# Two half-zero shifts of the first and of the last patch row share one operand

## The chip, the cores and the metric

The kernel runs on one core of a Trainium2 chip. The metric is the device time of one execution in microseconds. The engines are named as in the profile: PE (matrix products), PEld (its weight loads), DVE, ACT, POOL and SP; SP and ACT issue the DMAs.

## What is computed

The reference is a small vision tower. The first stage makes 5 images of 2 channels from each of 64 images of 104 x 104: the image itself and four copies shifted by 4 pixels in both directions and filled with zeros. They are normalised together, multiplied by gamma, moved by beta, and cut into 13 x 13 patches of 8 x 8, each patch giving 128 numbers. A class token is put in front, and two stages follow, of which the attention is a running state over the tokens.

```python
lu, ru, ld, rd = _shifts(x)
concat = jnp.concatenate((x, lu, ru, ld, rd), axis=1)
...
normed = (concat - mean) * jax.lax.rsqrt(var + EPS)
normed = normed * gamma[None] + beta[None]
y = jax.lax.conv_general_dilated(normed, W, window_strides=(PATCH, PATCH), padding='VALID', ...)
...
def step(S, qkv):
    qt, kt, vt = qkv
    S = S + LR * jnp.einsum('bd,be->de', vt, kt)
    out = jnp.einsum('de,be->bd', S, qt)
```

The two upward shifts have zeros in their last 4 pixel rows and the two downward shifts in their first 4. So in the first patch row (tokens 0 to 12) the upper half of a patch is zero in shifts 3 and 4, and in the last patch row (tokens 156 to 168) the lower half is zero in shifts 1 and 2. The last stage of the reference adds one-hot numbers beyond the 128 columns of the tower; here what is left of it is a layer norm that is added.

## The kernel before

**Tiles.** A token is one patch position for all 64 images, so 64 columns. Two tokens are a tile (85 tiles), four tiles a group (22 groups of 8 tokens, the last with one token). The 128 partitions hold the 128 pixels of a patch (2 channels, 64 pixels), in four blocks by quarter of the patch. Thus a half-zero patch is zero in 64 of the 128 partitions.

**Patch stage.** `rows` holds one row of windows in a slot (13 patches of the image itself and 14 shifted by half a patch, of which shifts 1 to 4 take 13 each, from this row or from the one above). `scale_shift` (L378) multiplies one row of one shift by its gammas into `scaled`, a ring of two rows: row 0 on DVE (L1006), all others on POOL (L1097). `conv` (L457) multiplies a piece of up to four tokens of one shift with the weights of that shift, into one of two PSUM banks; five shifts add up, and for groups from 5 on a product with `terms` (L469) adds beta and the image's mean. PE tells by `conv_step` that a shift of a group is done; ACT then copies the bank into `g_t` (`group_out`, L641), and POOL may overwrite the row.

**Head.** SP issues all first loads in one order (L407 to L421): gammas, row 0, the shifted windows above it (`first_offsets`), weights, the small matrices, row 1, beta, the images for the statistics with row 2 among them, and row 3 after DVE's scales of row 0. PE does groups 0 to 3 and part of 4, and the tables (L604) from which `terms` is made. ACT writes the tables to DRAM (`parked`, L767), SP waits for that (L423) and reads them back as `terms` (L427, L428). PE's `early` (L488) needs them; DVE adds its result to `g_t` (`whole`, L782), and ACT's `high` (L651) and POOL's `low` (L1099) split the sum in two parts.

**Steps.** From step -8 to step 71 every engine runs a list of work by step, four steps to a group, written out when the program is built. On PE a step holds the first half of its conv pieces, the three products `vr` (L499) of the tile four ahead, and the second half of the pieces. Every fourth step also has `turn` of the group two ahead (L490), and ends with `products` (L508) and `reads` (L524). On ACT it holds `high`, `values_out` (L665), `rows_out`, `finish`, and last `group_out` of the groups whose last piece lies in the step. `vr` of a tile writes the one bank `vr_ps` and so waits for ACT's `values_out` of the tile before it. On POOL a step holds `low` (first of four), `power` (last of four, L1104), and then the scales; `power(g)` computes 1/sqrt of the variances that DVE gives (L823, L865), and `values_out` of group g waits for it.

**The plan.** `late_item_step` (L86) spreads the 181 late conv pieces from step -8 on; from the 17th on a piece's step goes by the tokens ahead of it, up to step 71. `scale_step` (L134) puts a scale one step behind the last piece that read its place in the ring:

```python
    return int(sum(LATE_COST[sum(FIRST):i]) / sum(LATE_COST[sum(FIRST):]) * CONV_END)
...
    g = last_group_of_row(r - 2)
    steps = [st for (gi, si, _, _), st in zip(LATE_ITEMS, ITEM_STEPS) if gi == g and si == s]
    return 1 + max(steps)
```

After step 71 comes a tail written out by hand (L559). Its first `vr` and `turn` follow the last conv pieces directly.

Of the kernel before, what the change touches and what calls it, by code (L numbers as in the profile page):

```python
# [11 lines left out]
P = 128  # L12
B = 64
E = 128
S = 104
# [42 lines left out]
def tokens_of(g):  # L58
    return range(TOKENS * g, min(TOKENS * g + TOKENS, PATCHES))
# [5 lines left out]

def pieces(g):

    cuts, out = [tokens_of(g)[0], tokens_of(g)[-1] + 1], []
    cuts[1:1] = [t for t in tokens_of(g)[1:] if t % RING == 0]
    for a, z in zip(cuts, cuts[1:]):  # L70
        mid = a + (z - a + 1) // 2 if z - a > 4 else z
        out += [(a, mid - a)] + ([(mid, z - mid)] if mid < z else [])
    return out


def conv_items(g):
    return [(g, s, a, n) for s in range(SHIFTS) for a, n in pieces(g)]

# [63 lines left out]

LATE_SCALES = [(r, s, scale_step(r, s)) for r in range(EARLY_ROWS, N) for s in range(SHIFTS)]


def tower(nc, x_rows, x_windows, first_offsets, gamma, beta, weight, smalls, cls_tok, out, parked):
    with ExitStack() as ctx:
        def sb(name, shape, dtype=F32):
            return ctx.enter_context(nc.sbuf_tensor(name, shape, dtype))
# [4 lines left out]
        def sem(name):  # L154
            return ctx.enter_context(nc.semaphore(name))
# [4 lines left out]
        bet = sb("bet", [P, SHIFTS, PATCHES])  # L160
        wt = sb("wt", [P, SHIFTS, E])
        small = sb("small", [P, 8, E])
# [70 lines left out]
        gamma_in = sem("gamma_in")  # L233
        weight_in = sem("weight_in")
        beta_in = sem("beta_in")
        first_offsets_in = sem("first_offsets_in")
# [141 lines left out]
        def scale_shift(eng, r, s):  # L378
            offsets = (r if s < 3 else r - 1) % ROW_SLOTS
            right = N + (s - 1) % 2  # L380
            window = rows[:, r % ROW_SLOTS, 0:N] if s == 0 else rows[:, offsets, right:right + N]
            gains = gam[:, s, r * N:r * N + N].unsqueeze(2).to_broadcast([P, N, B])
            at = r % 2 * N
            return eng.tensor_tensor(scaled[:, s, at:at + N], window, gains, ALU.mult)  # L384
# [4 lines left out]
        def _(sp):  # L389
# [16 lines left out]

            sp.dma_start(gam[:], gamma).then_inc(gamma_in, 16)  # L407
            load_row(0)
            sp.dma_start(rows[:, ROW_SLOTS - 1, N:2 * N + 1], first_offsets).then_inc(first_offsets_in, 16)
            sp.dma_start(wt[:], weight).then_inc(weight_in, 16)  # L410
            sp.dma_start(small[:], smalls).then_inc(small_in, 16)
# [7 lines left out]

            sp.wait_ge(scaled_first, SHIFTS)  # L420
            load_row(3)  # L421
            sp.wait_ge(terms_zero, 1)
            sp.wait_ge(terms_parked, 32)  # L423
# [32 lines left out]
        def _(pe):  # L456
            def conv(item):  # L457
                g, s, a, n = item
                if s == 0 and a == tokens_of(g)[0] and g >= 2:
                    pe.wait_ge(g_ready, g - 1)  # L460
                wait_scaled(pe, s, a, n)
                at, first = (a - tokens_of(g)[0]) * B, s == 0 and a == tokens_of(g)[0]
                last = pe.matmul(conv_ps[g % 2][:, at:at + n * B], wt[:, s], scaled[:, s, a % RING:a % RING + n],  # L463
                                 start=first, stop=(g < EARLY and s == SHIFTS - 1), skip_group_check=True)
                if a + n == tokens_of(g)[-1] + 1:
                    last.then_inc(conv_step, 1)
                    if s == SHIFTS - 1 and g >= EARLY:
                        cols = len(tokens_of(g)) * B
                        pe.matmul(conv_ps[g % 2][:, 0:cols], terms[:, g], own_scales[:, 0:cols], start=False, stop=True,  # L469
                                  skip_group_check=True).then_inc(group_done, 1)  # L470
# [125 lines left out]
            pe.matmul(first_ps[:, 0:E], wq_c[:], small[:, MEM], start=True, stop=False, skip_group_check=True)  # L596
            pe.wait_ge(gamma_in, 16)
            pe.wait_ge(beta_in, 16)
# [182 lines left out]
        def _(dve):  # L781
# [221 lines left out]

            dve.wait_ge(gamma_in, 16)
            dve.wait_ge(row_in[0], 16)
            for s in range(SHIFTS):  # L1006
                if s == 3:
                    dve.wait_ge(first_offsets_in, 16)
                scale_shift(dve, 0, s).then_inc(scaled_first, 1)
# [81 lines left out]
        def _(pool):  # L1091
            def scale(r, s):
                if s == 0:
                    pool.wait_ge(row_in[r % ROW_SLOTS], 16 * (r // ROW_SLOTS + 1))
                if r >= 2:
                    pool.wait_ge(conv_step, SHIFTS * last_group_of_row(r - 2) + s + 1)
                scale_shift(pool, r, s).then_inc(scaled_rows, 1)  # L1097

# [57 lines left out]
            pool.tensor_tensor(cls_rho[:], cls_var[:], powers[:, 0:1], ALU.pow).then_inc(rho_ready, 1)  # L1156
            pool.wait_ge(gamma_in, 16)
            for r in range(1, EARLY_ROWS):
# [58 lines left out]
```

## Time and profile before

| | |
|---|---|
| median of 3 runs | 227.39 us (227.32 to 227.43) |
| the profiled execution | 227.42 us, of it 225.6 us from the first to the last instruction (span) |
| PE | busy 198.7 us, 88% |
| DVE | busy 152.6 us, 68% |
| ACT | busy 114.0 us, 51% |
| POOL | busy 160.1 us, 71% |
| conv products (L463) | 460 records, two for a piece, 116.0 us |
| scales on POOL (L384) | 60, 93.8 us, 1587 ns each |

The profile comes from one execution. A busy time is that of an engine's own instructions; waiting isn't counted. Products on PE overlap in their records, so what one costs is read from the chain of work, where the pieces follow one another without overlap. An idle time is written in brackets behind an instruction with what ended it. Of a chain, each piece is followed back from the last instruction to what released it.

### The profile page before, as it was taken

Reading aid. Unit: us, or ns where it says so; the run is one execution under the profiler, and the core shown is the slowest. Engines: PE = TensorE matmul, PEld = TensorE weight load, DVE = VectorE, ACT = ScalarE, POOL = GpSimd, SP = SyncE. Lnnn points to the kernel's source line nnn. Section 1 sums busy time; section 2 is a strip of 40 time slices with the busy share of each in tenths; the row PEclk is TensorE's granted clock in tenths of the full one; section 3 lists DMA queues with packets and bytes.
Section 4 is the critical chain, followed back from the end, with each engine's and each line's share of the span. In section 5 each row is a group of like instructions: output and inputs, shape, how many; then the busy total and the mean of one; then the engine's idle time right before and its main releaser. Section 6 shows DMA issues by size and latency. Waiting matters only on the chain.

```text
span 225.6 us, 4908 instructions
## 1 busy us (share of the span) xinstructions
PE 198.7 (88%) x1558; PEld 169.4 (75%) x1558; DVE 152.6 (68%) x752; ACT 114.0 (51%) x252; POOL 160.1 (71%) x126
## 2 busy tenths in 40 slices
PE   0299997899899999999999999999999999998700
PEld 0289896778788899888888888899888888887500
DVE  2558984251666876677695786588667769688771
ACT  6003211245344454656745666574567566467971
POOL 1039969899983799968999759849999353263550
PEclk9999999999999999999999999999999999999955
DMA  6999966922204004243044422022102202202255
GB/s 165 367 437 416 422 256 105 349 113 51 109 0 161 3 0 165 47 148 105 5 120 130 160 49 46 3 48 49 45 2 49 48 3 48 46 4 46 49 116 124
DMA packets 16527, 26.00 MB, mean 115 GB/s; under 512 B 1303, under 2 KB 13261, under 8 KB 16246
## 3 DMA queue, kind: packets, MB, share of 16 engines
q1 hardware_dynamic: 15820, 25.18, 34.9%
q10 hardware_dynamic: 682, 0.51, 0.7%
q8 instruction: 13, 0.21, 0.4%
q14 instruction: 12, 0.10, 0.1%
HBM read 19.77 MB, written 5.92 MB: 114 GB/s over the span
## 4 chain that ended last, share of the span: by engine, by line
PE 65%; DMA 12%; POOL 10%; DVE 6%; issue 2%; ACT 2%; POOLq 1%; SPq 0%; DVEq 0%; ACTq 0%
PE conv L463 29%; DMA rows<-x_windows 12%; PE vr_ps L505 11%; PE outs L532 9%; PE first_ps L515 8%; POOL scaled L384 7%; PE turn L495 4%; DVE scaled L384 2%; PE conv L469 2%; POOL g_low L1101 1%; PE conv L505 1%; ACT values L668 1%; POOL rstd L1111 1%; DVE state L811 1%; DVE state L803 1%
## 5 line engine op out<-in xcount | busy, mean ns | idle before, releaser
L463 PE MATMUL conv<-scaled,wt 128*128 128x256 f32 (+3 forms) x460 | 116.0, 372 | 9.9 <-DMA wt<-weight 9.9
L384 POOL TENSOR_TENSOR scaled<-rows,gam 128x832 f32<-128x832 f32 x60 | 93.8, 1587 | 6.3 <-PE conv L463 4.1
L463 PEld LDWEIGHTS conv<-scaled,wt 128*128 128x128 f32 x460 | 77.2, 193 | 18.0 <-DMA wt<-weight 9.9
L668 ACT ACTIVATE values<-vr_ps,rstd 128x256 f32<-128x256 f32 x78 | 36.9, 474 | 65.1 <-PE vr_ps L505 54.9
L1111 POOL TENSOR_TENSOR rstd<-var,powers 128x8 f32<-128x8 f32 (+2 forms) x20 | 30.4, 1519 | 23.9 <-DVE var L823 23.9
L803 DVE TENSOR_TENSOR state<-first_ps,state 128x128 f32<-128x128 f32 x80 | 23.3, 291 | 30.9 <-PE first_ps L515 26.1
L676 ACT ACTIVATE images<-images,ln_shift,ln_gain 128x128 f32<-128x128 f32 x82 | 38.0, 488 | 1.6 <-DVE ln_shift L874 1.6
L505 PE MATMUL vr_ps<-w_high,g_low 128*128 128x256 f32 x80 | 32.1, 401 | 0.2 <-ACT values L668 0.2
L1101 POOL TENSOR_TENSOR g_low<-g_t,g_high 128x512 fp32r<-128x512 f32 x21 | 26.8, 1275 | 5.1 <-ACT g_high L655 4.3
L792 DVE BATCH_NORM_STATS2 ln_stats<-images 128x6 f32<-128x128 f32 x85 | 23.7, 284 | 6.9 <-ACT images L662 6.7
L811 DVE TENSOR_TENSOR state<-second_ps,state 128x128 f32<-128x128 f32 x80 | 22.6, 282 | 2.1
L515 PEld LDWEIGHTS first_ps<-values 64*128 64x128 f32 x160 | 19.3, 187 | 6.2 <-issue 5.9
L515 PE MATMUL first_ps<-values 64*128 64x128 f32 x160 | 23.1, 284 | 0.2 <-ACT values L668 0.2
L518 PE MATMUL second_ps<-values 64*128 64x128 f32 x160 | 23.1, 285 | 0.0
L505 PE MATMUL vr_ps<-w_low,g_high 128*128 128x256 f32 x80 | 22.5, 281 | 0.0
L505 PE MATMUL vr_ps<-w_high,g_high 128*128 128x256 f32 x80 | 22.4, 280 | 0.0
L649 ACT COPY g_t<-conv 128x512 f32<-128x512 f32 (+1 forms) x22 | 12.3, 560 | 19.2 <-PE conv L463 19.2
L532 PE MATMUL outs<-state,g_t 128*64 128x128 f32 x304 | 20.8, 279 | 0.0
L832 DVE SCALAR_TENSOR_TENSOR images<-outs,rstd,images 128x128 f32<-128x128 f32 x72 | 20.4, 342 | 0.0
L505 PEld LDWEIGHTS vr_ps<-w_high,g_low 128*128 128x128 f32 x80 | 15.1, 189 | 6.1 <-issue 4.6
L518 PEld LDWEIGHTS second_ps<-values 64*128 64x128 f32 x160 | 19.3, 187 | 0.0
L840 DVE BATCH_NORM_STATS2 ln_stats<-images 128x6 f32<-128x128 f32 x85 | 18.9, 278 | 0.2 <-POOL images L1116 0.2
(149 smaller groups left out, 240.3 us busy)
## 6 DMA issues: line engine op xcount, KB each, us to landing
rows<-x_windows SPq DMA_DIRECT2D x13, 864.0 KB, 5.7
out<-images SPq DMA_DIRECT2D x40, 128.0 KB, 2.4
images<-x_rows SPq DMA_DIRECT2D x3, 624.0 KB, 22.0
images<-x_rows SPq DMA_DIRECT2D x1, 1456.0 KB, 13.1
images<-x_rows SPq DMA_DIRECT2D x1, 1248.0 KB, 15.5
images<-x_rows SPq DMA_DIRECT2D x1, 832.0 KB, 19.6
small<-smalls SPq DMA_DIRECT2D x1, 512.0 KB, 8.6
terms<-parked SPq DMA_DIRECT2D x3, 168.0 KB
```

The source lines that it names most:

```text
L384: return eng.tensor_tensor(scaled[:, s, at:at + N], window, gains, ALU.mult)
L463: last = pe.matmul(conv_ps[g % 2][:, at:at + n * B], wt[:, s], scaled[:, s, a % RING:a % RING + n], start=first, stop=(g < EARLY and s == ...
L505: last = pe.matmul(vr_bank(t)[:, 0:2 * E], x[:, at:at + E], w[:], start=(i == 0), stop=(i == 2))
L515: first = pe.matmul(first_bank[:, at:at + E], values[0:B, slot, 0], values[0:B, slot, 1], start=True, stop=True, skip_group_check=True)
L518: second = pe.matmul(second_bank[:, at:at + E], values[B:P, slot, 0], values[B:P, slot, 1], start=True, stop=True, skip_group_check=True)
L532: last = pe.matmul(out_bank(g)[a:a + B, at:at + E], g_t[:, g % G_SLOTS, at + a:at + a + B], state[:, t % STATE_SLOTS, half], start=True, s ...
L668: act.activation(values[:, t % VALUE_SLOTS].rearrange("p a e -> p (a e)"), vr_bank(t)[:, 0:2 * E], ACT.Identity, scale=rho_of(t)).then_inc ...
L676: return act.activation(tile_of(result, OUT_SLOTS, t), tile_of(h2, H2_SLOTS, t), ACT.Identity, scale=gain_of(t), bias=shift_of(t))
L803: dve.tensor_tensor(state[:, t % STATE_SLOTS, 0], banks_of(t)[0][:, at:at + E], state[:, (t - 1) % STATE_SLOTS, 1], ALU.add).then_inc(stat ...
L811: dve.tensor_tensor(state[:, t % STATE_SLOTS, 1], banks_of(t)[1][:, at:at + E], state[:, t % STATE_SLOTS, 0], ALU.add).then_inc(state_read ...
L1101: pool.tensor_tensor(low_of(g), g_t[:, g % G_SLOTS, 0:len(tiles_of(g)) * E], high_of(g), ALU.subtract).then_inc(low_ready, 1)
L1111: pool.tensor_tensor(rstd[:, g, 0:cols], var[:, g, 0:cols], powers[:, 0:cols], ALU.pow).then_inc(rho_ready, 1)
```

## The change

For tokens 0 to 12 shifts 3 and 4 are put together: their nonzero halves (64 partitions each) make one operand of 128 partitions, prepared on the host in `first_offsets`; a gamma row and a sixth set of weights are put together to match. For tokens 156 to 168 the same is done with shifts 1 and 2 (in the last row of `x_windows`, with a seventh set of weights). So these 26 tokens take four products instead of five. The pieces of shift 4 for the first row and of shift 2 for the last are gone, with one scale on DVE and one on POOL; some pieces are cut at token 13. The plan of pieces and scales is computed anew from the shorter list. SP issues two more DMAs: the put-together gammas (128 x 26 numbers) as the second of all, and the seventh set of weights (64 KB) behind row 3; the first load of weights has six sets instead of five. The waits on `gamma_in` count two loads, and PE waits on `bottom_in` before products with the seventh set. `conv_step` and `scaled_rows` count by two where one shift is gone.

```diff
@@ -63,10 +63,25 @@
-def pieces(g):
-
-    cuts, out = [tokens_of(g)[0], tokens_of(g)[-1] + 1], []
-    cuts[1:1] = [t for t in tokens_of(g)[1:] if t % RING == 0]
+TOP, BOTTOM = 3, 1
+LAST_ROW = N * (N - 1)
+
+
+def pieces(g, s):
+
+
+    a, z = tokens_of(g)[0], tokens_of(g)[-1] + 1
+    if s == TOP + 1:
+        a = max(a, N)
+    if s == BOTTOM + 1:
+        z = min(z, LAST_ROW)
+    if a >= z:
+        return []
+    cuts, out = [a, z], []
+    cuts[1:1] = [t for t in range(a + 1, z) if t % RING == 0 or (s == TOP and t == N)]
     for a, z in zip(cuts, cuts[1:]):
         mid = a + (z - a + 1) // 2 if z - a > 4 else z
         out += [(a, mid - a)] + ([(mid, z - mid)] if mid < z else [])
@@ -74,7 +89,7 @@
 def conv_items(g):
-    return [(g, s, a, n) for s in range(SHIFTS) for a, n in pieces(g)]
+    return [(g, s, a, n) for s in range(SHIFTS) for a, n in pieces(g, s)]
@@ -140,10 +155,11 @@
-LATE_SCALES = [(r, s, scale_step(r, s)) for r in range(EARLY_ROWS, N) for s in range(SHIFTS)]
+LATE_SCALES = [(r, s, scale_step(r, s)) for r in range(EARLY_ROWS, N) for s in range(SHIFTS)
+               if (r, s) != (N - 1, BOTTOM + 1)]
@@ -158,7 +174,8 @@
-        wt = sb("wt", [P, SHIFTS, E])
+        wt = sb("wt", [P, SHIFTS + 2, E])
+        gam_edges = sb("gam_edges", [P, 2, N])
@@ -379,7 +397,10 @@
-            gains = gam[:, s, r * N:r * N + N].unsqueeze(2).to_broadcast([P, N, B])
+            gains = gam[:, s, r * N:r * N + N]
+            if (r, s) in ((0, TOP), (N - 1, BOTTOM)):
+                gains = gam_edges[:, 1 if r else 0]
+            gains = gains.unsqueeze(2).to_broadcast([P, N, B])
@@ -405,9 +426,10 @@
             sp.dma_start(gam[:], gamma).then_inc(gamma_in, 16)
+            sp.dma_start(gam_edges[:], gamma_edges).then_inc(gamma_in, 16)
             load_row(0)
-            sp.dma_start(rows[:, ROW_SLOTS - 1, N:2 * N + 1], first_offsets).then_inc(first_offsets_in, 16)
-            sp.dma_start(wt[:], weight).then_inc(weight_in, 16)
+            sp.dma_start(rows[:, ROW_SLOTS - 1, N:2 * N], first_offsets).then_inc(first_offsets_in, 16)
+            sp.dma_start(wt[:, 0:SHIFTS + 1], weight[:, 0:SHIFTS + 1]).then_inc(weight_in, 16)
@@ -417,8 +439,9 @@
-            sp.wait_ge(scaled_first, SHIFTS)
+            sp.wait_ge(scaled_first, SHIFTS - 1)
             load_row(3)
+            sp.dma_start(wt[:, SHIFTS + 1], weight[:, SHIFTS + 1]).then_inc(bottom_in, 16)
@@ -460,10 +483,14 @@
-                last = pe.matmul(conv_ps[g % 2][:, at:at + n * B], wt[:, s], scaled[:, s, a % RING:a % RING + n],
-                                 start=first, stop=(g < EARLY and s == SHIFTS - 1), skip_group_check=True)
+                held = SHIFTS if s == TOP and a < N else SHIFTS + 1 if s == BOTTOM and a >= LAST_ROW else s
+                if held == SHIFTS + 1:
+                    pe.wait_ge(bottom_in, 16)
+                last = pe.matmul(conv_ps[g % 2][:, at:at + n * B], wt[:, held], scaled[:, s, a % RING:a % RING + n],
+                                 start=first, stop=(g < EARLY and (s == SHIFTS - 1 or held == SHIFTS)), skip_group_check=True)
                 if a + n == tokens_of(g)[-1] + 1:
-                    last.then_inc(conv_step, 1)
+
+                    last.then_inc(conv_step, 2 if (g, s) == (0, TOP) else 1)
@@ -1001,10 +1028,10 @@
-            dve.wait_ge(gamma_in, 16)
+            dve.wait_ge(gamma_in, 32)
             dve.wait_ge(row_in[0], 16)
-            for s in range(SHIFTS):
-                if s == 3:
+            for s in range(TOP + 1):
+                if s == TOP:
                     dve.wait_ge(first_offsets_in, 16)
                 scale_shift(dve, 0, s).then_inc(scaled_first, 1)
@@ -1094,7 +1121,7 @@
-                scale_shift(pool, r, s).then_inc(scaled_rows, 1)
+                scale_shift(pool, r, s).then_inc(scaled_rows, 2 if (r, s) == (N - 1, BOTTOM) else 1)
@@ -1187,6 +1214,17 @@
+    x_windows = np.concatenate([patches, offsets[:, 1:]], axis=2)
+    half = P // 2
+    x_windows[half:P, N - 1, N:2 * N] = offsets[0:half, N, 1:N + 1]
+    first_offsets = offsets[:, 0, 0:N].copy()
+    first_offsets[0:half] = offsets[half:P, 0, 1:N + 1]
```

## Rows read from the trace of the kernel before

**Rows 1.** Busy by stretch: PE, PEld, DVE, ACT, POOL; then PE clock, DMA share, GB/s.
```profile
66.00:196.00 130.00, 130.00 (x1079) 111.33 (x1077) 95.33 (x514) 75.15 (x167) 100.12 (x68) 1.00 0.23 64
...
27.00:42.00 15.00, 12.76 (x71) 11.16 (x70) 8.66 (x27) 2.05 (x5) 12.82 (x9) 1.00 0.73 214
```

**Rows 2.** Chain of work that ended last, the head: start us, us, what.
```profile
8.04 4.78 DVE scaled L384 x5
...
12.83 20.82 DMA rows<-x_windows
...
42.13 0.97 issue
```

**Rows 3.** PE's timeline and SP's wait before the first steps.
```profile
41.18 0.50 PE L488 MATMUL turn<-own_scales,terms 128*128 128x512 f32 x1 [0.92 <-DMA terms<-parked]
...
SPq L423 <- DMA parked<-term_parts: 22.0, 1, 22.0
```

**Rows 4.** The chain at the end of the loop, steps 69 to 72.
```profile
194.33 1.06 PE conv L463 x4
...
195.74 0.43 PE conv L463 x2
196.18 0.23 PE conv L469
196.41 0.61 PE conv L463 x6
197.02 0.41 PE vr_ps L505 x3
...
197.91 0.49 PE turn L495 x4
...
198.80 0.48 ACT values L668
...
199.41 0.34 PE first_ps L515
```

**Rows 5.** PE's timeline in the head: first product, and the wait for sums.
```profile
9.95 0.79 PE L463 MATMUL conv<-scaled,wt 128*128 128x256 f32 x1 [9.95 <-DMA wt<-weight]
...
34.67 0.38 PE L621 MATMUL outs<-sums,small 128*128 128x2 f32 x2 [0.40 <-DVE sums L1060]
```

**Rows 6.** Stretches in the head, columns as in rows 1; ACT queue's packets, MB, share.
```profile
9.00:14.00 5.00, 4.05 (x10) 3.25 (x11) 4.96 (x13) 0.00 (x0) 0.00 (x0) 1.00 1.05 434
...
31.60:33.70 2.10, 2.10 (x17) 2.10 (x16) 2.07 (x7) 0.59 (x1) 0.00 (x0) 1.00 0.12 49
...
q10 hardware_dynamic: 224, 0.03, 1.9%
```

**Rows 7.** POOL's timeline in the first burst of scales; DVE's variance before it.
```profile
74.89 1.58 POOL L384 TENSOR_TENSOR scaled<-rows,gam 128x832 f32<-128x832 f32 x1 [3.63 <-PE conv L463]
76.43 1.79 POOL L1111 TENSOR_TENSOR rstd<-var,powers 128x9 f32<-128x9 f32 x1
...
94.58 1.63 POOL L1111 TENSOR_TENSOR rstd<-var,powers 128x8 f32<-128x8 f32 x1
...
75.98 0.28 DVE L823 TENSOR_SCALAR var<-dve,powers,moments 128x4 f32<-128x4 f32 x1
```

**Rows 8.** ACT's wait for power; vr(25) in the chain; two starts after a wait.
```profile
96.31 0.47 ACT L668 ACTIVATE values<-vr_ps,rstd 128x256 f32<-128x256 f32 x1 [1.84 <-POOL rstd L1111]
...
97.90 0.35 PE vr_ps L505 x3
...
206.09 0.59 PE conv L505 x3
...
60.58 0.65 PE L495 MATMUL turn<-small,g_t 128*128 128x128 f32 x4 [0.64 <-DVE g_t L786]
```

**Rows 9.** ACT's timeline in step 69.
```profile
196.15 0.48 ACT L676 ACTIVATE images<-images,ln_shift,ln_gain 128x128 f32<-128x128 f32 x1
196.54 0.57 ACT L649 COPY g_t<-conv 128x512 f32<-128x512 f32 x1
```

More of the change, by code:

```diff
@@ L140, in scale_step, with tower @@
     return 1 + max(steps)
-LATE_SCALES = [(r, s, scale_step(r, s)) for r in range(EARLY_ROWS, N) for s in range(SHIFTS)]
-def tower(nc, x_rows, x_windows, first_offsets, gamma, beta, weight, smalls, cls_tok, out, parked):
+LATE_SCALES = [(r, s, scale_step(r, s)) for r in range(EARLY_ROWS, N) for s in range(SHIFTS)
+               if (r, s) != (N - 1, BOTTOM + 1)]
+def tower(nc, x_rows, x_windows, first_offsets, gamma, gamma_edges, beta, weight, smalls, cls_tok, out, parked):
     with ExitStack() as ctx:
@@ L234, in tower @@
         weight_in = sem("weight_in")
+        bottom_in = sem("bottom_in")
         beta_in = sem("beta_in")
@@ L596, in _ @@
             pe.matmul(first_ps[:, 0:E], wq_c[:], small[:, MEM], start=True, stop=False, skip_group_check=True)
-            pe.wait_ge(gamma_in, 16)
+            pe.wait_ge(gamma_in, 32)
             pe.wait_ge(beta_in, 16)
@@ L1156, in _ @@
             pool.tensor_tensor(cls_rho[:], cls_var[:], powers[:, 0:1], ALU.pow).then_inc(rho_ready, 1)
-            pool.wait_ge(gamma_in, 16)
+            pool.wait_ge(gamma_in, 32)
             for r in range(1, EARLY_ROWS):
@@ L1189 @@
             offsets[q:q + 32, 1 - a:1 - a + N, 1 - b:1 - b + N] = patches[src:src + 32]
+    x_windows = np.concatenate([patches, offsets[:, 1:]], axis=2)
[3 more added lines that the diff above has]
+    first_offsets[0:half] = offsets[half:P, 0, 1:N + 1]
+    gains = windows(gamma.reshape(SHIFTS, 2, S, S)).reshape(P, SHIFTS, PATCHES)
+    weight = w.reshape(E, SHIFTS, 2, 2, HALF, 2, HALF).transpose(3, 5, 2, 4, 6, 1, 0).reshape(P, SHIFTS, E)
+    gain_edges = [np.concatenate([gains[half:P, TOP + 1, 0:N], gains[half:P, TOP, 0:N]]),
+                  np.concatenate([gains[0:half, BOTTOM, LAST_ROW:], gains[0:half, BOTTOM + 1, LAST_ROW:]])]
+    weight_edges = [np.concatenate([weight[half:P, TOP + 1], weight[half:P, TOP]]),
+                    np.concatenate([weight[0:half, BOTTOM], weight[0:half, BOTTOM + 1]])]
     smalls = np.zeros((P, 8, E), np.float32)
@@ L1198 @@
         "x_rows": x.reshape(P, S, S),
-        "x_windows": np.concatenate([patches, offsets[:, 1:]], axis=2),
-        "first_offsets": offsets[:, 0],
-        "gamma": windows(gamma.reshape(SHIFTS, 2, S, S)).reshape(P, SHIFTS, PATCHES),
+        "x_windows": x_windows,
+        "first_offsets": first_offsets,
+        "gamma": gains,
+        "gamma_edges": np.stack(gain_edges, axis=1),
         "beta": windows(beta.reshape(SHIFTS, 2, S, S)).reshape(P, SHIFTS, PATCHES),
-        "weight": w.reshape(E, SHIFTS, 2, 2, HALF, 2, HALF).transpose(3, 5, 2, 4, 6, 1, 0).reshape(P, SHIFTS, E),
+        "weight": np.concatenate([weight, np.stack(weight_edges, axis=1)], axis=1),
         "smalls": smalls,
```

## Prediction, made before the changed kernel was run

> **What bounds the kernel now.** I read the page's busy shares first, then busy time by stretch, then the chain of work that ended last, then the timelines of single engines where the change touches them. The picture has three parts. From 66 to 196 us PE is busy in 130.00 of 130.00 us [rows 1]: what is taken off PE there comes off the time, as long as nobody makes PE wait. Before that PE has gaps (12.76 of 15.00 us from 27 to 42) [rows 1], and the chain starts from DMA: row 3 of the windows lands at 12.83 + 20.82 = 33.65 us, and POOL scales it [rows 2]. The piece to look at is the 0.97 us from 42.13: POOL has finished its scales and stands for the first `g_high`. That comes from PE's first `early` product at 41.18 us, which waited 0.92 us for the DMA of `terms`, and SP could issue that DMA only after 22.0 us of waiting for the `parked` writes [rows 3]. So the landing of `parked` and `terms` sets the start of the steps, and row 3 has some 1.0 us to spare behind it. The third part, after 196 us, starts from PE's last turns and `vr` products and follows them one to one.
>
> **Head, PE and DVE.** Group 0 loses its two products of shift 4; group 1 loses one and gets smaller ones. A piece of 4 tokens costs 0.43 us [rows 4], 0.107 a token, so 13 tokens are 1.4 us of PE. DVE loses one scale (five took 4.78) [rows 2], and as `cls_var` comes behind them, POOL starts row 1 some 0.95 us earlier. None of it reaches the start: PE then waits longer for `sums` at 34.67 us [rows 5], which hangs on the last image chunk, and POOL waits longer for row 3. I count zero. The cover is the DMA stream; without it this would be worth up to 1.4 us.
>
> **Head, DMA.** SP's queue gets a load of 13 KB in 104-byte pieces ahead of row 0, 64 KB more weights ahead of `small`, and 32 KB less of `first_offsets`: 45 KB more ahead of the images and row 3, at 434 GB/s [rows 6] 0.1 us. The nearest row for small packets are the 224 packets of the ACT queue: 1.9% of 16 engines over 10 us, 13.6 ns each [rows 6]; 8 per engine are 0.1 us. The Trainium skill (DMA: Bandwidth & Descriptors, Specifications) wants at least 512 B for line rate and calls anything less a read-modify-write; it gives no price for one, and the row above says that these are cheap. Row 0 is issued one slot later, but the gamma load ahead of it is still in flight then. The other 64 KB (the weights for row 12) are queued behind row 3 and meet the `parked` writes. From 31.6 to 33.7 us only 49 GB/s flow, at a DMA share of 0.12: about two of the 16 engines still work off a backlog [rows 6]. If the load spreads over 16, a late engine gets 4 KB more, 0.16 us at 49/2 GB/s. If all 64 KB had to pass at 49 GB/s, it would be 1.3 us. I take 0.3 for the whole, bounds 0.1 and 1.5. It stands in front of `terms`, so it is paid in full. Row 3 is issued after four scales instead of five, but it spends 20.8 us in the queue anyway: nothing.
>
> **Loop, PE.** The planner spreads the late pieces evenly by tokens up to step 71: 669 tokens and 181 pieces before, 656 and 177 after; three pieces of four tokens and one of one token vanish. By both plans, worked out from the code, 12 tokens are gone by the start of step 69: 3 x 0.43 = 1.29 us, in a stretch where PE has no gap. This is the gain. The single token goes in step 70.
>
> **Loop, POOL.** The plan also moves POOL's scales, whose step is that of a conv piece plus one. (6,0) goes from step 10 to step 11, where it stands behind `power(4)` in POOL's order. Before, it ran at 74.89 us, in the time before DVE gave the variance of group 4 (75.98 + 0.28), and POOL was then busy without a gap until `power(6)` ended near 96.18 us [rows 7]. Up to that `power` the instructions are the same before and after; only the start differs. PE is 0.43 us ahead by then (step 7 has one piece less), so `power(4)` starts at 75.85 and the pair is done at 79.15 instead of 78.21, and `power(6)` ends 0.94 us later, at 97.12. ACT's `values` of tile 24 waited 1.84 us for it already and began at 96.31 [rows 8]. After: 97.25, done 97.72, seen by PE 0.13 later (ACT's end 199.28 to PE's 199.41 [rows 4]) at 97.85. `vr(25)` ran from 97.90 for 0.35 us [rows 8]; 0.43 earlier it would end at 97.82. Starting at 97.85 after a wait it ends at 98.44 (three took 0.59 so [rows 8]). So PE stands about 0.62 us, with all of step 21 queued behind it, and as PE has no gap later, nothing makes it up. Bounds 0 (POOL gets its variance earlier than I think) and 0.9. The other bursts: (8,0) also goes a step later, but its piece lies in the first half of step 24, and `power(10)` comes 0.4 us later, within the 0.65 us or so that `vr(25)` had beyond the longest wait of before; rows 10 to 12 have fewer scales ahead of their powers than before. Zero for these. (12,2) is gone, 1.54 us of POOL near 165 us, where PE is the bound: nothing.
>
> **End of the loop.** The last piece of group 20 moves from step 69 to step 70. ACT's order in step 70 is `values(74)`, then the copies of groups 20 and 21. PE's is that piece, the bias product, two single tokens, `vr(74)`, two single tokens, then `turn(20)`, which needs the copy of group 20. So the copy comes behind `vr(74)`; before, it ran at 196.54 [rows 9], while `vr(74)` ended at 197.43 [rows 4]. From the start of step 69 to the end of that turn it was 197.91 + 0.49 - 194.33 = 4.07 us [rows 4]. After, by the same rows: 0.63 (half of the two pieces at 194.33, with the start after reads), 0.35 and 0.43 for step 69; 0.43, 0.23, 0.41 (two of three single tokens in 0.61) and 0.41 to the end of `vr(74)`; 0.04 to ACT, 0.39 to the copy (one step on ACT [rows 9]), 0.57 for it, 0.13 to PE, and 0.65 for a turn after a wait [rows 8]. Sum 4.67: 0.60 longer, where 0.21 shorter was to be had. Bounds -0.21 and 0.7. Behind the turn comes `vr(75)`, then `values(75)` at 198.80, for which PE stood before 199.41 [rows 4], so the tail takes it in full.
>
> **The sum.** The profiled execution took 227.42 us, span 225.6 and 1.8 around it; the median of the runs is 227.39, and 0.03 is not worth a correction. 227.42 + 0.3 (DMA) - 1.29 (pieces) + 0.62 (`power(6)`) + 0.60 (step 70) = 227.65.
>
> **The rivals.** A measurement of this kernel can tell about 0.2%, 0.45 us, from no change; "same" is 226.95 to 227.85.
> First, the forecast: the two new waits and the DMA eat the pieces. 227.65. Chance 0.45.
> Second, the gain arrives. Both waits rest on differences of half a microsecond; with neither, 227.42 - 1.49 + 0.1 = 226.0; with the step-70 wait alone and 0.3 of DMA 227.0, and 226.6 with half of it. For it: PE stood nowhere in 130 us though ACT waited up to 1.84 us for `power` [rows 1, 8]. Against it: both waits follow from the order of the instructions. Chance 0.27.
> Third, slower: the 64 KB behind row 3 hold up the `parked` writes. The place is the thin stream after 31.6 us, the price up to 1.3 us instead of 0.16, and it decides from a start that comes 0.5 us later: 227.42 + 1.5 - 1.29 + 0.62 + 0.60 = 228.85, at half the price 228.3. For it: the stream is thin because few engines carry it [rows 6]. Against it: the weights can spread over all 16. Chance 0.22.
> Fourth, PE's rate. The first product after 9.95 us of rest took 0.79 us [rows 5], nearly twice the 0.43 that two of them take later, and the change leaves PE without work for about 1.8 us before `sums` (0.40 before), longer than the 0.92 before `early` [rows 3, 5]. At half rate the six pieces after `sums` (16 tokens) take 3.4 us instead of 1.7 and the four after them as much again; they end near 42.3 us, some 1.1 after the landing of `terms`: 228.75. The Trainium skill (TensorE: Matmul & The Clock Gate, Part 1) says that an idle array falls to half its 2.4 GHz clock and gets it back only after sustained work; the profile's own column grants 1.00 from 9 to 14 us as elsewhere [rows 1, 6], so the trace shows the long product and not its cause. Chance 0.03.
> Fifth, it does less than it says: a piece's price is that of its two weight loads, not of its tokens. Pieces of four at 0.43 against single tokens at 0.20 [rows 4] speak against it; with 4 late pieces less at 0.20 the sum is 228.1. Chance 0.03.
>
> **How the numbers follow.** Slower: 0.22, 0.03 and 0.03, less what of the third lies under 227.85: 0.27. Faster: 0.26 of the second's 0.27. Same: 0.47. The range goes from half of the step-70 wait to half the price of the slower rival, about 1 in 10 outside at either end.
>
> **What would show it.** Right: PE's first gap in the loop is near 97 us, at `vr` and for ACT's `values`, 0.3 to 0.9 us, with ACT waiting about 3.2 us for `rstd` (1.84 + 0.94, and PE 0.43 earlier); `turn(20)` waits for ACT's copy about 0.65 us; `early(0)` starts between 41.3 and 41.8 us; conv pieces take 2.8 us less in all. Wrong: `early(0)` at 42 us or later (third); PE without a gap from 66 us to the last turn (second); conv products near 0.8 us after `sums` (fourth). The forecast as a whole is wrong if the copy of group 20 runs ahead of `vr(74)`, or if `power(4)` finds its variance ready.

## The result and the profile after

The changed kernel takes 229.84 us (median of 22 runs, 228.07 to 232.36) where the kernel before takes 227.30 us beside it (22 runs, 227.19 to 227.91): the ratio is 1.0098, 95% interval 1.0079 to 1.0117. Two of its runs (231.87 and 232.36 us) lie over 1.5% above its fastest, count as slow and are left out of the ratio. It is slower by 1%, outside the predicted range (226.6 to 228.3 us), and its times spread over 4 us where those of before spread over 0.7. The profiled execution took 230.41 us, span 228.6: 2.99 us more than that of before.

The page of the profile after gives, as engine, busy time, share of the span and instructions, and as the granted clock by slices in tenths:

```profile
PE 198.0 (87%) x1546; PEld 168.2 (74%) x1546; DVE 152.2 (67%) x751; ACT 113.8 (50%) x252; POOL 158.6 (69%) x125
PEclk9999999799999999999999999999999999999975
```

PE and POOL have less work than before (198.7 and 160.1 us), so the loss is not work. The eighth slice of the clock, a 7, is the stretch from 40.0 to 45.7 us; it was a 9 before. The chain of work that ended last (start, us, what) shows where it lies:

```profile
5.81 12.81 DMA images<-x_rows
...
18.64 3.42 DVE dve L1066 x8
22.06 1.24 DVE w_low L1069
...
27.25 9.09 DMA parked<-term_parts
...
38.28 4.94 DMA terms<-parked
43.27 0.79 PE turn L515
...
64.04 0.66 PE turn L522 x4
...
101.17 0.57 PE vr_ps L532 x3
...
196.86 0.63 PE conv L489 x2
```

Of before, the same turn starts at 60.58 [rows 8] and the same pieces at 194.33 [rows 4]. So the kernel is 3.46 us late at the turn, has won back 0.93 at the pieces with which step 69 begins (2.53 late), and loses 0.5 in step 70. The whole question is the head. PE's timeline there (start, us, line, operation, partitions and elements; idle before in brackets), and then one line of before:

```profile
35.04 0.38 PE L648 MATMUL outs<-sums,small 128*128 128x2 f32 x2 [1.03 <-DVE sums L1087]
...
43.27 0.79 PE L515 MATMUL turn<-own_scales,terms 128*128 128x512 f32 x1 [3.41 <-DMA terms<-parked]
43.86 2.61 PE L489 MATMUL conv<-scaled,wt 128*128 128x256 f32 x6
```

```profile
41.52 1.46 PE L463 MATMUL conv<-scaled,wt 128*128 128x256 f32 x6
```

`early(0)` starts at 43.27 instead of 41.18, after 3.41 us of waiting for `terms` instead of 0.92 [rows 3]. And the six products behind it take 2.61 us; the same six took 1.46 before. The view by microsecond (length; busy us and instructions of PE, PEld, DVE, ACT and POOL; granted clock, DMA share, GB/s) says why:

```profile
42.00:43.00 1.00, 0.00 (x0) 0.00 (x0) 0.00 (x0) 0.00 (x0) 0.00 (x0) 0.88 0.76 194
43.00:44.00 1.00, 0.73 (x2) 0.64 (x3) 0.00 (x0) 0.00 (x0) 0.00 (x0) 0.50 0.94 387
...
45.00:46.00 1.00, 1.00 (x4) 0.72 (x4) 0.00 (x0) 0.44 (x1) 0.48 (x1) 0.50 0.99 408
46.00:47.00 1.00, 1.00 (x8) 0.89 (x7) 0.00 (x0) 0.06 (x1) 1.00 (x2) 0.91 1.06 436
```

From 43 to 46 us PE is granted 0.50, which is the lower of its two levels (1.2 of 2.4 GHz), after its long rest. The lateness of 3.46 us at the turn is thus 2.09 from the later start of `early(0)` and 1.37 from what follows it. The Trainium skill (TensorE: Matmul & The Clock Gate, Part 1) says that an idle array falls to half its 2.4 GHz clock; the trace agrees, with 0.50 granted after 3.41 us of rest.

The later start has two parts. The first `terms` load is issued 1.23 us later (35.20 and 36.43), behind a `parked` that was issued 1.41 us later (25.47 before, 26.88 after). From there to `early(0)` it takes 6.84 us instead of 5.98, 0.86 more. The second is the surprise: nothing in the change touches that transfer. Of the first, about 1 us is not seen in every execution: e4_warm and e7_plan below have the same head up to that point, and there the load is issued at 35.41 and 35.56. Why it came at 36.43 here (and at 36.29 in e2_late) stays open.

### The profile page after: what moved, and what is told of

Read it like the earlier page. It is cut to its first block, busy times and chain, and to the rows that moved or that the text cites. A ratio compares the mean times of both kernels' runs of the same rounds, so it can differ in the third digit from the quotient of the medians.

```text
span 228.6 us, 4888 instructions
## 1 busy us (share of the span) xinstructions
PE 198.0 (87%) x1546; PEld 168.2 (74%) x1546; DVE 152.2 (67%) x751; ACT 113.8 (50%) x252; POOL 158.6 (69%) x125
## 4 chain that ended last, share of the span: by engine, by line
PE 65%; DMA 12%; DVE 8%; POOL 5%; SPq 3%; ACT 3%; issue 2%; POOLq 1%; DVEq 0%; ACTq 0%
PE conv L489 29%; PE vr_ps L532 11%; PE outs L559 9%; PE first_ps L542 8%; DMA images<-x_rows 6%; DMA parked<-term_parts 4%; PE turn L522 4%; DVE dve L1066 3%; POOL scaled L405 3%; DMA terms<-parked 2%; PE conv L496 2%; PE conv L532 1%; POOL rstd L1138 1%; ACT values L695 1%; DVE state L838 1%
## 5 line engine op out<-in xcount | busy, mean ns | idle before, releaser
L489 PE MATMUL conv<-scaled,wt 128*128 128x256 f32 (+3 forms) x448 | 114.8, 375 | 10.8 <-DMA wt<-weight 10.8
L405 POOL TENSOR_TENSOR scaled<-rows,gam 128x832 f32<-128x832 f32 x58 | 90.5, 1583 | 2.9 <-DMA rows<-x_windows 1.5
L489 PEld LDWEIGHTS conv<-scaled,wt 128*128 128x128 f32 x448 | 75.7, 195 | 18.9 <-DMA wt<-weight 10.8
```

The lines of the kernel that those rows point to most:

```text
L489: last = pe.matmul(conv_ps[g % 2][:, at:at + n * B], wt[:, held], scaled[:, s, a % RING:a % RING + n], start=first, stop=(g < EARLY and (s ...
```

## The experiments

In all tables here "issue" is SP's issue of the first `terms` load, and "early" the start of `early(0)`. Ratios are to the kernel before, run beside each, with the 95% interval; they are not those of the two medians. A time inside a kernel is that of its one profiled execution.

| | median us (range, runs) | ratio | issue to early | PE's rest before it |
|---|---|---|---|---|
| before | 227.30 (227.19–227.91, 22) | | 35.20 → 41.18: 5.98 | 0.92 |
| after | 229.84 (228.07–232.36, 22) | 1.0098 [1.0079, 1.0117] | 36.43 → 43.27: 6.84 | 3.41 |
| e1_fold | 228.81 (227.51–230.71, 12) | 1.0068 [1.0043, 1.0093] | 35.47 → 42.32: 6.85 | 2.13 |
| e2_late | 228.28 (227.76–230.96, 12) | 1.0061 [1.0034, 1.0087] | 36.29 → 43.27: 6.98 | 2.83 |
| e3_fold_late | 229.38 (227.66–230.15, 12) | 1.0077 [1.0055, 1.0100] | 35.32 → 42.37: 7.05 | 2.08 |
| e4_warm | 228.59 (228.44–228.86, 5) | 1.0056 [1.0044, 1.0068] | 35.41 → 42.65: 7.24, not all of it the load | none |
| e5_before_edges | 229.09 (228.04–231.37, 9) | 1.0091 [1.0054, 1.0127] | 35.28 → 42.43: 7.15 | 1.89 |
| e6_before_bottom | 227.38 (226.85–227.58, 11) | 1.0001 [0.9993, 1.0010] | 35.16 → 41.15: 5.99 | 0.87 |
| e7_plan | 228.93 (227.56–230.08, 7) | 1.0068 [1.0040, 1.0096] | 35.56 → 42.56: 7.00 | 2.17 |
| e8_all | 227.88 (227.26–229.34, 12) | 1.0047 [1.0028, 1.0066] | 35.32 → 42.24: 6.92 | 2.00 |
| f1_sbuf | 229.28 (227.99–230.32, 7) | 1.0083 [1.0053, 1.0113] | 35.13 → 42.44: 7.31 | 2.43 |
| f2_dram | 227.31 (227.08–227.59, 11) | 1.0000 [0.9991, 1.0008] | 35.14 → 41.15: 6.01 | 0.93 |
| f3_all_sbuf | 226.75 (226.29–226.83, 7) | 0.9970 [0.9959, 0.9980] | 35.26 → 41.23: 5.97 | 0.87 |
| f4_all_both | 226.18 (226.12–226.80, 5) | 0.9962 [0.9949, 0.9974] | 35.29 → 41.17: 5.88 | 0.99 |
| g1_pad | 227.28 (227.16–227.44, 11) | 1.0003 [0.9994, 1.0011] | 35.72 → 41.53: 5.81 | 1.24 |
| g2_pad_plan | 226.88 (226.72–226.99, 11) | 0.9983 [0.9975, 0.9992] | 35.48 → 41.44: 5.96 | 1.48 |
| g3_shift256 | 227.22 (227.18–227.40, 11) | 1.0001 [0.9992, 1.0009] | 35.13 → 40.96: 5.83 | 0.69 |
| g4_terms_only | 229.74 (227.97–230.56, 6) | 1.0098 [1.0068, 1.0128] | 35.10 → 41.79: 6.69 | 1.70 |

### The two added transfers, taken away one by one

The first suspects were the two new loads. e1_fold puts the 26 gammas behind the others, in one tile and one load; e2_late moves the weights for the last row behind row 4, after all of `terms`; e3_fold_late does both.

```diff
-        gam = sb("gam", [P, SHIFTS, PATCHES])
-        gam_edges = sb("gam_edges", [P, 2, N])
+        gam_all = sb("gam_all", [P, SHIFTS * PATCHES + 2 * N])
...
-            sp.dma_start(gam[:], gamma).then_inc(gamma_in, 16)
-            sp.dma_start(gam_edges[:], gamma_edges).then_inc(gamma_in, 16)
+            sp.dma_start(gam_all[:], gamma).then_inc(gamma_in, 16)
```

> The changed kernel, with the 13 KB of put-together gammas appended to the gamma load, so that no small DMA stands second in SP's queue. Theory A (the small DMA holds back the first loads: row 0 landed 0.8 us later, the first images 0.8 us later, DMA moved 55 GB/s from 4 to 5 us instead of 248; through the tables and the parked writes this delays terms, and PE rests until its clock falls): row 0 lands at 8.0 us again, early(0) starts near 41.5 us, no stretch at half clock, 227.2 to 227.6. Rival B (the 64 KB behind row 3 hold up the parked writes): no change, 229.8. Rival C (the longer wait for terms is chance of the DMA, not tied to an edit): 228 to 232 again.

```diff
             load_row(3)
-            sp.dma_start(wt[:, SHIFTS + 1], weight[:, SHIFTS + 1]).then_inc(bottom_in, 16)
...
             load_row(4)
+            sp.dma_start(wt[:, SHIFTS + 1], weight[:, SHIFTS + 1]).then_inc(bottom_in, 16)
```

> The changed kernel, with the 64 KB of weights for the last row loaded behind row 4, after the terms, instead of behind row 3. Theory A (small DMA ahead of row 0): parked done at 36.4 us as before, early(0) near 43 us, 229.5 or more. Rival B (these 64 KB hold up the parked writes): parked lands 0.5 to 1.2 us earlier, early(0) near 41.8 us, 227.8 to 228.3.

> Both edits of e1_fold and e2_late. Theory A: as e1_fold within 0.3 us, 227.0 to 227.6. Rival B: as e2_late. If both matter, clearly under either: the head is that of the kernel before, and the time is 227.4 - 1.3 + 0.2 (power) + 0.5 (step 70) = 226.8.

All three stay slower than before. e2's median lies where its rival B put it (227.8 to 228.3), but not for B's reason: B wanted `early(0)` near 41.8, and it comes at 43.27. The fold brings row 0 at 8.16 instead of 8.84. `terms` is issued 0.96 us earlier than in after; that this is the fold's doing isn't shown, since e4_warm, without the fold, issues it at 35.41 too. And `early(0)` comes only at 42.32, since the transfer itself takes 6.85 us. With both loads out of the way (e3), issue stands at 35.32, as good as before's 35.20, and `early(0)` is still 1.19 us late.

### The clock

e4_warm gives PE ten products whose result is not used, just ahead of the wait for `terms`; the rest is after.

```diff
+            for _ in range(10):
+                pe.matmul(vr_ps[:, 2 * E:3 * E], wq_c[:], small[:, MEM], start=True, stop=True, skip_group_check=True)
             pe.wait_ge(terms_in, 16 * 2 * PRODUCTS)
```

> The changed kernel, with ten products of 128 columns that nobody reads on PE before its wait for terms, some 2.2 us of work in a rest of 3.4 us. If the fall of the clock after that rest is a part of the loss (0.50 granted from 43 to 46 us, three pieces in 2.6 us instead of 1.5), then no stretch at half clock, and 1.1 to 1.4 us less: 228.4 to 228.7, with less spread. If the clock cost nothing because DVE or POOL was late anyway: 229.8.

PE's timeline of e4_warm:

```profile
40.50 2.40 PE L660 MATMUL vr_ps<-small,wq_c 128*128 128x128 f32 x20
...
42.65 0.48 PE L515 MATMUL turn<-own_scales,terms 128*128 128x512 f32 x1
42.96 1.46 PE L489 MATMUL conv<-scaled,wt 128*128 128x256 f32 x6
```

The products are at the upper level again, 1.46 us for six instead of 2.61, and the spread of the times is gone: 0.4 us over five runs instead of 4. So the halved clock is real, and without it the spread is gone, in these five runs. Yet the kernel is still 0.56% slower than before: the late `terms` is not explained by the clock. e4 also starts `early(0)` 0.62 us sooner than after does, since its `terms` is issued at 35.41. It pays something of its own as well: `early(0)` follows the unused products without idle time, and the last of the six loads lands at 42.16, so about half a microsecond of its 7.24 is those products and not the load, which takes 6.75.

### One part alone, on the kernel before

e5_before_edges gives the kernel before the small gamma tile and its load, which nobody reads (the waits on `gamma_in` count it, as in the changed kernel); e6_before_bottom gives it 64 KB of weights behind row 3.

```diff
+        gam_edges = sb("gam_edges", [P, 2, N])
...
+            sp.dma_start(gam_edges[:], gamma_edges).then_inc(gamma_in, 16)
```

> The kernel before, with one more DMA of 13 KB (104 bytes a partition) second in SP's queue, which nothing uses. Theory A (it holds back the first loads and so terms): row 0 lands 0.8 us later, early(0) 1 to 2 us later, the clock falls in some executions, 228.5 to 231 with a spread of 2 us or more. Rival B (the other load is to blame): 227.4, no spread.

```diff
+        wt_more = sb("wt_more", [P, E])
...
             load_row(3)
+            sp.dma_start(wt_more[:], weight[:, SHIFTS]).then_inc(bottom_in, 16)
```

> The kernel before, with one more DMA of 64 KB behind row 3, which nothing uses. Theory A: 227.3 to 227.6. Rival B (it holds up the parked writes): 0.5 to 1.5 us more, 227.9 to 228.9.

```profile
42.43 0.50 PE L490 MATMUL turn<-own_scales,terms 128*128 128x512 f32 x1 [1.89 <-DMA terms<-parked]
```

```profile
41.15 0.50 PE L491 MATMUL turn<-own_scales,terms 128*128 128x512 f32 x1 [0.87 <-DMA terms<-parked]
```

The first line is of e5, the second of e6. The 64 KB cost nothing: 41.15 against 41.18. The small tile brings nearly the whole loss, 0.91% of 0.98%. But e5 issues `terms` at 35.28, on time; it is again the transfer that takes 7.15 us. A load of 13 KB from the start of the kernel, over 25 us earlier, is hardly in its way. What the tile leaves behind is 104 bytes a partition, 128 as the tiles are laid out, and all tiles behind it move up by them.

### The plan

e7_plan is after with the pace of the late pieces as it was before, so that every scale, and every piece up to group 18, has the step that it had before; e8_all has it along with fold and late load.

```diff
-CONV_END = 71
+CONV_END = 71 * 592 / 605
```

> The changed kernel, with the plan's end scaled down with the tokens (71 x 592 / 605 = 69.5), so that every piece up to group 18 and every scale has the step it had in the kernel before, and group 20 is done in step 68. If the new steps cost 0.2 us at vr(25) and 0.5 at turn(20), as the trace of the changed kernel reads: 0.7 to 0.8 us less than the changed kernel, 229.1, with no wait of PE for ACT's copy and none for power near step 21. If that time comes back elsewhere: 229.8.

> The changed kernel with the gammas in one load, the last weights behind row 4 and the scaled plan. Sum of the parts: 227.4 for the head of before, less 1.3 to 1.5 for the pieces, no new waits: 225.9 to 226.2. If the head stays late from another cause (64 KB more weights ahead of the images): 226.5 to 227.5.

e8_all misses its 225.9 to 226.2 by 1.7 us. Both kernels still have the late `terms`; e8_all, in an execution where the clock didn't fall (2.00 us of rest, 1.00 granted), reached 227.26. What the plan is worth shows only in g2_pad_plan, below.

### Where a tile lies

Worked out from the order of the tiles, `terms` starts 180224 bytes into a partition before, a multiple of 512, and 181376 after, 128 bytes beyond one. A partition's row of one `terms` load is 512 bytes. f1_sbuf is the kernel before with 104 unused bytes, and no load. f2_dram leaves the tiles alone and makes the gammas' array in DRAM as much longer.

```diff
         bet = sb("bet", [P, SHIFTS, PATCHES])
+        unused = sb("unused", [P, 2 * N])
```

> The kernel before, with 104 bytes a partition of SBUF set aside behind beta and used by nothing, so that the tiles behind it (weights, small matrices, scaled, terms and the rest) lie 104 bytes higher, as in the changed kernel. In the seven profiles so far with such a shift, terms came 6.8 to 7.2 us after SP's issue; in the two without, 6.0. Theory D (the place of the tiles in SBUF sets the DMA's pace): terms 6.8 us or more after issue, PE's rest about 1 us longer, 227.8 to 229 with more spread, with no added DMA at all. Rival E (the place of parked in DRAM, or the added DMA): 227.3.

> The kernel before, with the gamma array in DRAM 13 KB longer (104 bytes a partition, not loaded), so that what lies behind it in DRAM is moved as in the changed kernel. Rival E (place in DRAM): terms 6.8 us or more after issue, 227.8 or more. Theory D (place in SBUF): 6.0 us, 227.3.

```profile
35.13 0.33 SPq L428 DMA_DIRECT2D terms<-parked  x1
```

```profile
42.44 0.56 PE L489 MATMUL turn<-own_scales,terms 128*128 128x512 f32 x1 [2.43 <-DMA terms<-parked]
42.80 2.76 PE L464 MATMUL conv<-scaled,wt 128*128 128x256 f32 x6
```

This is f1: a program that does exactly what before does, with 104 bytes between two tiles, loses 0.83%. `terms` is issued at 35.13 and lands 7.31 us later; the six products behind it take 2.76 us. f2 is at 1.0000. DMA share and GB/s by microsecond (after the comma: granted clock, share, GB/s), first of f1, then of before:

```profile
37.00:38.00 1.00, 1.00 1.18 115
38.00:39.00 1.00, 1.00 1.28 104
39.00:40.00 1.00, 1.00 1.28 90
40.00:41.00 1.00, 1.00 1.55 143
```

```profile
37.00:38.00 1.00, 1.00 0.97 170
38.00:39.00 1.00, 1.00 1.28 116
39.00:40.00 1.00, 1.00 1.52 184
40.00:41.00 1.00, 1.00 0.75 207
```

Over the four microseconds the DMA engines are busier in f1 (mean share 1.32 against 1.13) and move less (113 GB/s against 169). The packets themselves say it most plainly. The six loads are 1014 packets of 512 bytes; in the DMA records of f1 one takes 74 ns on average, in those of before 52.

g4_terms_only leaves the tiles ahead of `terms` where they were and puts `terms` 104 bytes further (to 128 beyond a multiple of 512, since this kernel's tiles start at multiples of 32). Its expectation says that every other tile keeps its place against 512; that isn't quite so. The 408 bytes behind `terms` take 416, and `term_parts` and what follows it start 32 bytes beyond such a multiple. g3_shift256 moves it, and all behind, by 256 bytes. g1_pad is after with the small tile made 512 bytes long, of which 104 are used.

```diff
+        unused = sb("unused", [P, 26])
         terms = sb("terms", [P, GROUPS, E], F32R)
+        unused_too = sb("unused_too", [P, E - 26])
```

> The kernel before, with 104 unused bytes ahead of terms and 408 behind it: terms alone starts 128 bytes beyond a multiple of 512, every other tile keeps its place against 512. If terms is the tile that matters: 6.8 us or more from issue to early(0), 228 to 230 as in f1_sbuf. If it is another tile (small, weights, scaled, rows of values): 6.0 us and 227.3.

```diff
         bet = sb("bet", [P, SHIFTS, PATCHES])
+        unused = sb("unused", [P, 64])
```

> The kernel before, with 256 unused bytes a partition behind beta, so that weights, terms and the rest start 256 bytes beyond a multiple of 512. If a row must not straddle a multiple of 512: terms 6.8 us or more after issue and 228 to 230, as in f1_sbuf (128 beyond). If multiples of 256 are enough: 6.0 us and 227.3.

```diff
-        gam_edges = sb("gam_edges", [P, 2, N])
+        gam_edges = sb("gam_edges", [P, E])[:, 0:2 * N].rearrange("p (k t) -> p k t", t=N)
```

> The changed kernel with one edit: the tile of the put-together gammas takes 512 bytes a partition instead of 104, so that terms and all behind it start at a multiple of 512 bytes again (181760 instead of 181376; 181376 is 128 more than such a multiple). Nothing else moves, the small DMA stays. Theory D (512-byte rows that straddle a multiple of 512): terms 6.0 us after SP's issue instead of 6.8. Row 0 and the tables are still late, so early(0) near 42.2 us, 227.6 to 228.2; if the clock still falls in some executions, spread. Rival A (the small DMA makes all of the loss): 229.8.

`early(0)` in g4, g3 and g1, one fence each, and behind g1's the six products:

```profile
41.79 0.50 PE L490 MATMUL turn<-own_scales,terms 128*128 128x512 f32 x1 [1.70 <-DMA terms<-parked]
```

```profile
40.96 0.50 PE L489 MATMUL turn<-own_scales,terms 128*128 128x512 f32 x1 [0.69 <-DMA terms<-parked]
```

```profile
41.53 0.50 PE L515 MATMUL turn<-own_scales,terms 128*128 128x512 f32 x1 [1.24 <-DMA terms<-parked]
41.87 1.46 PE L489 MATMUL conv<-scaled,wt 128*128 128x256 f32 x6
```

Moving `terms` gives the whole loss (1.0098, the ratio of after). The 32 bytes of the tiles behind it don't touch the six loads, which come from DRAM and write `terms`; `parked`, which is written from `term_parts`, goes out at 25.36 and lets `terms` be issued at 35.10, as early as in any kernel here. The profiled execution of g4, at 227.97 us the fastest of its six, kept the clock at 1.00 and so shows the price of the late landing by itself: 0.61 us. The other 1.8 us of its median (229.74) came in executions of which there is no trace; after's trace puts 1.37 us on the clock, and some 0.4 us of g4 stay untraced. A shift of 256 bytes costs nothing (1.0001), and g1 takes the whole loss off the change: 1.0003, better than the 227.6 to 228.2 us expected of it. In the table all runs in which `terms` starts 96 or 128 bytes beyond a multiple of 256 (after, e1 to e5, e7, e8, f1, g4) need 6.69 to 7.31 us from issue to `early(0)`, and all others 5.81 to 6.01. Their 512-byte packets take 62 to 74 ns on average, those of the others 48 to 52. The Trainium skill (DMA: Bandwidth & Descriptors, How a descriptor splits into AXI transactions) says of reads that a transaction must start at a multiple of 256 bytes, and that a transfer which starts between two of them fetches bytes that it doesn't use. Taken over to the writes here, that would make three transactions of a 512-byte row instead of two, an estimate. The runs agree in where the border lies (96 and 128 cost, 256 doesn't); they don't show transactions, nor does the page give a price in time.

### What the change is worth with its tile in place

f3_all_sbuf is e8_all with the gamma tile lengthened to keep `terms` at a multiple of 512, f4_all_both has the gammas' rows in DRAM lengthened too; g2_pad_plan is g1 with the plan of e7.

```diff
-        gam_all = sb("gam_all", [P, SHIFTS * PATCHES + 2 * N])
+        gam_all = sb("gam_all", [P, SHIFTS * PATCHES + E])
```

> The changed kernel as in e8_all (gammas in one load, last weights behind row 4, scaled plan), with the put-together gammas in a tile that is 512 bytes longer instead of 104, so that the tiles behind it move by a multiple of 512. Theory D: terms 6.0 us after issue, no stretch at half clock, 225.9 to 226.6, little spread. Rival E: as e8_all, 227.3 to 229.3.

> As f3_all_sbuf, and the gamma array in DRAM is also longer by 512 bytes a partition (64 KB) instead of 13 KB. Theory D: as f3_all_sbuf. Rival E: only this one has terms 6.0 us after issue, and 225.9 to 226.6. If neither: 227.3 to 229.3, and the cause of the late terms is still open.

> As g1_pad, and the scaled plan. Against g1_pad this prices the new steps of scales and pieces: 0.7 us less (0.2 at vr(25), 0.5 at turn(20)). Against f4_all_both and f3_all_sbuf it prices the separate small DMA with its late row 0: 0.5 to 1 us more than they. If the plan's waits had been swallowed elsewhere: as g1_pad.

f3 lands 0.15 us above the 225.9 to 226.6 us that were expected, f4 within them; g2, expected 0.5 to 1 us above the two, lies 0.13 and 0.70 above. f4_all_both, at 226.18 us, is faster than both kernels: 0.38% below before and 3.7 us below after. f3 and f4 each show values near 226.2 or 226.3 and near 226.8; whether the longer rows in DRAM shift them from one to the other isn't settled. The plan is worth 0.40 us (227.28 to 226.88). The two waits that it takes away cost 0.22 and 0.50 us (next section), 0.72 together. The chain of g2 shows where a part of the rest went:

```profile
195.41 0.42 PE vr_ps L532 x3
...
195.86 0.48 ACT values L695
...
196.48 0.61 PE vr_ps L532 x3
...
197.11 0.48 ACT values L695
...
197.73 0.61 PE vr_ps L532 x3
```

With the last pieces done by then, nothing lies between one `vr` and the next, and each waits for ACT's `values`: 1.25 us from the second to the third.

## Why the prediction was wrong

**Head, PE and DVE.** Counted at zero, and right. PE waited 1.03 us for `sums` instead of 0.40 [rows 5], hidden behind `terms`.

**Head, DMA: the step that failed.** I took 0.3 us, bounds 0.1 to 1.5, for the bytes and packets added, and took the transfer of `terms` itself as unchanged. `early(0)` came 2.09 us late, and the clock added 1.37. Of the 2.09, 0.86 is the longer transfer, and the runs show its cause, the place of the tile; 1.23 is the later issue, most of which two other executions with this head don't have. The two loads themselves were not badly priced in their effect: in g1_pad and g2_pad_plan, which have them both, `early(0)` is 0.35 and 0.26 us late. They do more upstream than I said, though. Row 0 lands 0.8 us later (DVE's first scale at 8.84, before 8.04 [rows 2]), against my 0.1, and in the fifth microsecond only 55 GB/s flow:

```profile
4.00:5.00 1.00, 1.00 0.32 55
```

Before it was 248 GB/s at a share of 0.89. DVE's `w_low` took 1.33 us where it took 0.73, and with the late row 0 that makes the 1.41 us by which `parked` went later in after. `w_low` isn't the loads' doing: it took 1.21 and 1.11 us in e1 and e3, which haven't got the small load, and 0.75 in e5, which has it and not the change. What in the change does it, no run isolates. g1 has the same delays (row 0 at 9.15, `w_low` 1.39 us, `parked` issued at 27.19) and loses little by them: from that issue to the one of `terms` it takes 8.53 us, where before takes 9.73. What I didn't ask at all is what a new tile does to the tiles behind it. It was in the diff, one line, and I costed its load and not its place. None of the five rivals had it; the third, with the right effect and the right time (`early(0)` at 42 us or later), named the 64 KB behind row 3, and e6_before_bottom shows those free.

**The clock.** The fourth rival had the mechanism, at a chance of 0.03, and at the wrong place: I looked at the rest before `sums`, where after's trace grants 1.00, and not at the one before `early`, which grows with every delay of `terms`. A late `terms` can be paid twice, once as the wait and again as half a clock for some 3 us. Only the profiled executions show the fall itself. That it comes in some executions of a kernel and not in others is read from the times: in after, executions at a mean granted clock of 0.975 or more took 228.07 to 228.75 us, but for one of 230.00; those at 0.970 or less 229.56 or more. The profiled one, with its fall, stands between them at 0.974 and 230.41 us. What took three others to between 231 and 232.4 us, no trace shows.

**Pieces, -1.29.** Right in kind: from the turn to the pieces of step 69 after needs 0.93 us less than before. Of the 0.36 us missing, the wait of the next point takes 0.22; 0.14 stays open.

**`power(6)`, +0.62.** The mechanism is right, its size not. ACT's timeline, then POOL's:

```profile
100.53 0.47 ACT L695 ACTIVATE values<-vr_ps,rstd 128x256 f32<-128x256 f32 x1 [2.80 <-POOL rstd L1138]
```

```profile
98.80 1.63 POOL L1138 TENSOR_TENSOR rstd<-var,powers 128x8 f32<-128x8 f32 x1
```

ACT waited 2.80 us (3.2 predicted) and PE's `vr` behind it, in the chain shown first, took 0.57 us instead of 0.35. That is 0.22 us. By my sum ACT's wait was to grow from 1.84 us by 1.37 (POOL 0.94 later, PE 0.43 sooner); it grew by 0.96, and the 0.41 between them is the error of the term. 0.18 of it is POOL's: `power(6)` starts at 98.80 where it started at 94.58 [rows 7], which is 0.76 us beyond the 3.46 of the turn, and not 0.94. The other 0.23 stays open.

**Step 70, +0.60.** Right. PE's timeline:

```profile
200.77 0.66 PE L522 MATMUL turn<-small,g_t 128*128 128x128 f32 x4 [0.56 <-ACT g_t L676]
```

I said that `turn(20)` would wait about 0.65 us for ACT's copy of group 20; it waited 0.56. From the start of step 69 to the end of that turn it took 201.43 - 196.86 = 4.57 us, 4.67 predicted, 4.07 before [rows 4].

**The sum.** g1_pad is the change without the fault of its tile: 227.28 us, where 227.65 was forecast, and the two waits eat much of what the pieces give, as said. That it lands so near is in part luck, since `power(6)` cost 0.4 us less than forecast and the pieces gave less. So the argument about the loop held in kind, and the result was decided by a line that it left out.

## What to carry to other kernels

Before a tile is added, work out where the tiles behind it come to lie: one that a DMA on the critical path fills in short rows should keep its start at a multiple of 256 bytes, and padding the new small tile to 512 bytes cost nothing here (g1_pad). When a profile shows a known transfer longer though its issue is on time, test the place with an unused tile in the old kernel before looking for a rival transfer. And where PE rests ahead of a wait that sets the end, a late landing may be paid a second time through the clock; here the first sign was a spread of the times.

## What the runs showed of the hardware

- 512-byte rows written into SBUF from 96 or 128 bytes beyond a multiple of 256: 6.69 to 7.31 us from the first issue of the six loads to the use of their data, against 5.81 to 6.01 us at multiples of 256 (the changed kernel, 16 experiments and the kernel before). A packet of 512 bytes takes 62 to 74 ns on average in the first, 48 to 52 in the second. Other offsets were not tried.
- The granted clock fell to 0.50 after rests of 1.89 (e5), 2.08 (e3), 2.13 (e1), 2.17 (e7), 2.43 (f1), 2.83 (e2) and 3.41 us (after), and stayed at 1.00 after 1.24 (g1), 1.48 (g2), 1.70 (g4) and 2.00 us (e8). The length of the rest alone doesn't decide: it fell after 1.89 and not after 2.00.
- A load of 13 KB in 104-byte pieces, second in the queue, delays row 0 behind it by 0.8 us in after and by 0.97 in e5 (9.01 instead of 8.04), by 0.5 to 1.1 us over the seven kernels that have it (0.5 in g2, 1.1 in g1), where the 224 small packets of another queue [rows 6] had suggested 0.1.
